# Expert layer of a four-layer Perceiver step: the down products of a pair of experts ordered by their number of rows

## What is computed

```python
B, S, H = (1, 256, 256)
E, K, I = (16, 4, 176)      # 16 experts, 4 per token, inner width 176
IS = 352                    # shared expert, here cut into 2 of width 176
CAP = 128                   # tokens that an expert takes
# for every expert e:
#   mid = silu(x @ w_gate[e]) * (x @ w_up[e])       256 x 176
#   out += weight[token, e] * (mid @ w_down[e])     256 x 256
```

## Time and profile before

| | before |
|---|---|
| runs | 1710.92, 1711.04, 1713.58 us |
| profiled execution, its own time | 1710.72 us |
| its span (first to last instruction) | 1709.0 us |
| TensorE busy, share of the span | 92% |
| VectorE | 61% |
| ScalarE | 46% |
| GpSimd | 32% |
| stage `l0_ffn` in the span | 437 to 537 us |

### The profile page before, as it was taken

The page is one execution under the profiler, slowest core; times in us unless marked ns, Lnnn a source line. Parts: engine busy times, 40 slices in busy tenths (PEclk is TensorE's granted clock), DMA queues, the critical chain, the costliest instruction groups (busy, mean ns, idle before and its releaser), DMA issues. The chain is left out here.

```text
span 1709.0 us, 27646 instructions
## 1 busy us (share of the span) xinstructions
PE 1564.5 (92%) x9976; PEld 1096.9 (64%) x9976; DVE 1044.1 (61%) x2120; ACT 791.1 (46%) x2197; POOL 549.5 (32%) x647
## 2 busy tenths in 40 slices
PE   7989999997899789998789999999999898999969
PEld 5655555554565547787567877777878545666657
DVE  5786666642566556664445665454453379999963
ACT  2223555554112336335433443433443378999931
POOL 2263445452000000431332242242240007777720
PEclk9988999998899989998799999999999999999979
DMA  3000000003233141400100000000000253333110
GB/s 136 1 11 16 2 2 2 2 2 140 104 112 122 31 93 38 132 1 1 50 1 1 1 1 1 1 1 1 2 1 1 94 160 102 110 117 115 41 60 22
DMA packets 53549, 78.04 MB, mean 46 GB/s; under 512 B 14755, under 2 KB 31139, under 8 KB 52518
## 3 DMA queue, kind: packets, MB, share of 16 engines
q1 hardware_dynamic: 53414, 76.27, 13.8%
HBM read 76.00 MB, written 0.26 MB: 45 GB/s over the span
## 5 line engine op out<-in xcount | busy, mean ns | idle before, releaser
L718 DVE TENSOR_REDUCE x_row_max<-banks 128x1 f32<-128x512 f32 x256 | 164.8, 686 | 88.4 <-PE banks L406 88.4
L663 ACT ACTIVATE x_v_full<-banks 128x512 f32<-128x512 f32 x256 | 138.9, 595 | 119.2 <-PE banks L435 118.1
L605 POOL CAST x_v_full<-x_v_full 128x1024 int16<-128x1024 f32 x128 | 133.2, 1040 | 142.8 <-ACT x_v_full L663 141.7
L406 PE MATMUL banks<-x_kT,x_qT 32*128 32x512 f32 x512 | 159.8, 670 | 4.0 <-DVE x_row_max L718 3.5
L2539 PE MATMUL banks<-x_v,ctx_tokens 128*128 128x128 f32 x1088 | 148.7, 277 | 10.9 <-ACT ctx_tokens L2704 5.9
L213 PE MATMUL banks<-a_w_ring,x_normed_T 128*128 128x512 f32 x320 | 146.7, 598 | 4.8 <-DVE a_r L3311 4.8
L435 PE MATMUL banks<-x_qT_shifted,x_kT 32*128 32x256 f32 x1024 | 145.6, 401 | 0.0
L2539 PEld LDWEIGHTS banks<-x_v,ctx_tokens 128*128 128x128 f32 x1088 | 134.0, 192 | 15.7 <-ACT ctx_tokens L2704 7.3
L2628 POOL TENSOR_TENSOR ctx_tokens<-ctx_tokens 128x512 f32<-128x512 f32 (+1 forms) x48 | 54.4, 1133 | 231.9 <-DVE ctx_tokens L2769 231.9
L2787 DVE TENSOR_REDUCE x_small<-banks 128x1 f32<-128x2048 f32 x32 | 73.3, 2292 | 86.9 <-PE banks L2520 86.9
L2520 PE MATMUL banks<-x_kT,ctx_tokens 128*128 128x512 f32 x256 | 119.0, 609 | 4.3 <-ACT x_exps L2686 4.3
(11 more groups left out here) (536 smaller groups left out, 3454.4 us busy)
## 6 DMA issues: line engine op xcount, KB each, us to landing
a_w_ring<-in_L_attn_WB_T SPq DMA_DIRECT2D x16, 512.0 KB, 3.7
a_w_ring<-in_L_attn_WC_T SPq DMA_DIRECT2D x16, 512.0 KB, 5.3
f_gate_up<-in_L_ffn_gate_up SPq DMA_DIRECT2D x9, 736.0 KB, 4.2
ctx_tokens<-in_ctx SPq DMA_DIRECT2D x16, 256.0 KB, 6.0
a_w_ring<-in_L_attn_Wth_T SPq DMA_DIRECT2D x8, 512.0 KB, 4.0
a_bias_ring<-in_L_attn_B_bias_perm SPq DMA_DIRECT2D x16, 256.0 KB, 4.9
a_bias_ring<-in_L_attn_C_bias_perm SPq DMA_DIRECT2D x16, 256.0 KB, 6.0
f_w_down<-in_L_ffn_down SPq DMA_DIRECT2D x9, 384.0 KB, 4.8
```

What stands on the lines that cost most here:

```text
L406: return nc.tensor.matmul(k.bank(bank), qt[lo:lo + SLOT, g, b * T:(b + 1) * T], kt[lo:lo + SLOT, g, HALF * i:HALF * (i + 1)], start=True, ...
L605: nc.gpsimd.tensor_copy(er[q % 4], ew[q % 4]).then_inc(s.rounded, 1)
L663: nc.scalar.activation(ew[q % 4][:, e * HALF:(e + 1) * HALF], k.bank(score_bank(n)), ACT.Exp).then_inc(s.scores_taken, 1)
L718: nc.vector.reduce_max(mx[:, p % 2, e, b, i:i + 1], k.bank(bank), AX.X).then_inc(taken, 1)
```

## The change

`down` now takes a pair instead of an expert. It queues first the four products over 128 rows (expert 0 and 1, both sequences), then the four over 48 rows, which alternate between the two experts: the even expert's operands lie in partitions 0 to 47 and go to bank 6, the odd one's in partitions 64 to 111 and go to bank 7. Only the first product into a bank clears it. The waits go with it: the pair waits once, at its head, for `out_taken` of the whole pair before it (`2 * B * p`), and pair 0 waits for `count_taken` at its head. Both experts signal `out_in_psum` at the end of the pair.

```diff
-                def down(e):
-                    p = e // 2
+                def down(p):
                     pe.wait_ge(s.mid_ready, p + 1)
                     pe.wait_ge(down_loaded[p % PAIR_RING], 16 * (p // PAIR_RING + 1))
-                    if e >= 2:
-                        pe.wait_ge(s.out_taken, B * (e - 1))
-                    if e == 1:
+                    if p >= 1:
+                        pe.wait_ge(s.out_taken, 2 * B * p)
+                    else:
                         pe.wait_ge(s.count_taken, 1)
+                    for e in range(2):
+                        for b in range(B):
+                            nc.tensor.matmul(k.bank(6 + e, P, D, b * D), mid[:, p % 2, e, b * T:(b + 1) * T], wd[:, p % PAIR_RING, e], start=(b == 0), stop=False)
                     for b in range(B):
-                        sl = slice(b * T, (b + 1) * T)
-                        last = matmul_acc(nc, k.bank(6 + e % 2, P, D, b * D),
-                                          [(mid[:, p % 2, e % 2, sl], wd[:, p % PAIR_RING, e % 2]),
-                                           (rest[rows(e), p % 2, sl], wd[rows(e), p % PAIR_RING, 2])])
-                    last.then_inc(s.out_in_psum, 1)
+                        for e in range(2):
+                            last = nc.tensor.matmul(k.bank(6 + e, P, D, b * D), rest[rows(e), p % 2, b * T:(b + 1) * T], wd[rows(e), p % PAIR_RING, 2], start=False, stop=(b == B - 1))
+                            if b == B - 1:
+                                last.then_inc(s.out_in_psum, 1)
                 for p in range(npair):
                     gate_up(p)
...
                     if p >= 1:
-                        down(2 * p - 2)
-                        down(2 * p - 1)
-                down(ne - 2)
-                down(ne - 1)
+                        down(p - 1)
+                down(npair - 1)
```

## The result

The changed kernel took 1696.77 us in the median of three executions (1695.61 to 1697.63 us) against 1711.74 us for the kernel before in the same measurement: ratio 0.9914, 95% interval 0.9898 to 0.9931. Two executions, a fourth of the changed kernel (1732.4 us) and one in experiment 8 (3898.83 us), were disturbed and are left out of every median, range and ratio in this document. The forecast was 1696.4 us.

A forecast was written before the change was run, and what follows sets the result against it. TensorE's own queue was taken to pace the stage. Nine pairs save 18.4 us; less waits of 0.8, 2.0, 0.8 and a longer first step, 14.6 us, giving 1696.4 us, range 1692.5 to 1702.5 (8 in 10).

The forecast's parts named there:

- A pair's down products: 128-row products 1.81 us plus 48-row products 1.07 us, 2.88 in place of 4.92 us per pair, 2.04 us less.
- The row of the other stage: Trace row of eight 64-row instructions in two partition halves and two banks, going in pairs: 1.07 us, taken for 48 rows.
- First pair: The first pair's head waits for the token count, so TensorE starts its down products about 0.8 us later.
- Last pair: With no gate_up between, four takes stand between pair 7's end and pair 8's head: 2.0 us lost.
- End: Four takes instead of the last expert's stand behind the last matmul, and the next layer norm waits: 0.8 us lost.
- The sum: Nine pairs save 18.4 us, less 0.8, 2.0 and 0.8, and a longer first step: 14.6 us gained.
- Middle pairs and VectorE: Four takes finish under the next gate_up with 3.5 us of cover; VectorE's longest turn, 7.6 us, fits the 8.16 us period.
- Strict order: Rival: matmul starts strictly in order, five steps instead of four, 0.22 us more per pair, 1698.3 us; 5 in 100.
- no overlap: Rival: the two experts' 48-row products do not overlap, 1.93 instead of 1.07 us per pair, 1704.1 us; 6 in 100.
- a passage between the halves: Rival: passing between partition halves costs as much as between 128 and 48 rows, 1709.3 us; 2 in 100.
- The fall of the clock at the standstill: Clock falls before the last pair, doubling its 2.6 us of matmuls, 1699 us; with the first case 84 in 100.
- rival 5: Clock falls at the stage's end and stays low in the next, up to some 25 us more, about 1721; 3 in 100.

The follow-up runs named there:

- experiment 8: The kernels of experiment 5 and experiment 7 once more, unedited, side by side: 1694.71 us and 1691.77 us.
- Experiment 4: Kernel before, with only each expert's two 128-row products queued ahead of its two 48-row ones, waits per expert as before: 1704.32 us, ratio 0.9958.
- experiment 3: Changed kernel with TensorE waiting for the even expert's 48-row products to complete before the odd ones: 1705.68 us, ratio 0.9968.
- experiment 6: Changed kernel with pair 0's wait for the token count put back before the odd expert's first product: 1698.53 us, ratio 0.9924.
- experiment 5: Changed kernel with the last pair's down products in banks 3 and 4, without the wait for the previous pair's takes: 1692.12 us, ratio 0.9889.
- experiment 2: Changed kernel with the four 48-row products queued even, even, odd, odd instead of alternating: 1696.5 us, ratio 0.9917.
- change_again: The changed kernel measured a second time, without edit, for its profile: 1697.04 us in the median of five, ratio 0.9917.
- late_count: The kernel of experiment 6, the changed kernel with pair 0 waiting later for the token count: 1698.53 us, ratio 0.9924.
- experiment 7: Changed kernel with the edits of experiment 5 and experiment 6 together: 1695.42 us, ratio 0.9903.

## Why the prediction was right

**A pair's down products**, forecast 1.81 + 1.07 = 2.88 us, measured 2.88. The period, forecast 8.16, measured 8.17. The row of the other stage was the right nearest row: 48 rows go together in pairs like 64. Experiment 4 shows the passages' part of the 2.04 us apart (0.79 for four of them, so about 1.2 for the six that are gone), experiment 3 that the overlap, the other 0.86, is real.

**First pair**, forecast 0.8 us lost, measured 0.87 (1.67 against 0.80 from the last `gate_up` instruction to the first down product); experiment 6 took it back.

**Last pair**, forecast 2.0, of which 0.1 is a longer first step. Measured 1.9 by the gap, and 1.90 us instead of 1.82 for the eight instructions behind it; experiment 5 shortened the stage by 1.9.

**End**, forecast 0.8: four takes begin at 519.89 and the layer norm at 521.87, 1.98 us; before it was 1.20 (536.41 to 537.61). 0.78 us.

**The sum**, forecast 14.6. From the last `gate_up` instruction of pair 1 to the layer norm it is 68.75 us against 83.5: 14.8. Ahead of that the changed kernel was already 1.0 us earlier, 0.8 of it in the first two `gate_up`: the code is the same there, and the granted clock between 441 and 458 us was 0.90 against 0.84. That is no effect of the change.

**Middle pairs and VectorE.** Forecast 7.6 us of work in 8.16. The shortest wait of VectorE for a pair's products is 0.70 us, so its longest turn took 7.5 us, and TensorE waited for VectorE only where forecast. The reloads were hidden, as forecast: in the stage the `f_gate_up` ones landed 4.0 to 4.6 us after their issue. The 8.3 us in the earlier trace rows, which the forecast passed over and which would not fit in a period, belongs to a first load ahead of the stage.

**The rivals.** Strict order, no overlap and a passage between the halves were out by the period alone, and experiment 2 puts the first aside with an order that would have made it plain. The fall of the clock at the standstill did not come in the profiles of `change_again` and of experiment 2. It did come in that of experiment 6, whose stage began 0.4 us later, and in that of the 1732.4 us (0.50 from 532.3 us, in the middle of its last pair): two of four profiles with that standstill, so the forecast had reason to allow for it. Its price of 2.6 us was too high, 1.7 measured, since only part of the pair ran at the low level. What the forecast named only as part of rival 5, a slower kernel, and put at nothing in the likeliest case, is the fall in the next stage: it came, at 523 us, for 7 us, and cost 2.5 us in `l1_xattn`. It went into the allowance of 2.5 us for shifts in later stages, and shifts the other way (1.0 us ahead of the down products, 1.7 us behind `l1_xattn`) hid it in the total. So the sum of 14.6 us was right by its terms, against 14.8 in the stage; that the total came within 1 us of the forecast is in part luck.

## What to carry to other kernels

Queue products by their number of rows: in this kernel a product over 48 rows between two over 128 brought 0.4 us of passages, 0.2 each, and 0.2 us is about one matmul instruction of 256 columns. Put two products over 48 or 64 rows, the two cases seen here, in the two halves of the partitions and in two banks; the second one is then free, in whatever order the halves are queued. Other numbers of rows, and both in one bank, were not tried. When outputs of two units are joined so that both end together, look at the place with no other work between (here the last pair and the end of the stage): the takes come to stand on the path there, and a bank that is free by then removes the wait.

## What the runs showed of the hardware that was not expected

Halves of the partitions do not wait for each other's place in the queue (experiment 2). A standstill of 1.9 us before the last pair let the granted clock fall in one kernel (`late_count`, 0.50 from 518.2 us) and not in another with the same standstill (`change_again`). An idle time of 2.0 us behind the stage, unfilled, was followed by a fall of some 3 to 7 us in the next stage in the profiles of `change_again` and of experiments 2, 5, 6, 7 and 8, so in every one of these six; in experiment 3 it came after 1.23 us, and in the kernel before and in experiment 4, with the same 1.2 us, it did not. Five products over the gap prevented it in two profiles, three products in the one looked at. And executions of one kernel differ by up to 5 us with no reason in its code. One reason in the clock is seen: in the profile of experiment 7 it stayed at the 1.2 GHz level for longer in the first stage (0.58 between 118 and 155 us, 0.68 in the others), and that stage, the same in all kernels, took 405 us instead of 401.
